# Last stage of two Fourier layers on one core: tile copies and plane loads issued by GpSimd's queue instead of the sync engine's

## The reference, cut to what matters

```python
# layer 0: 16 x 16 Fourier modes, plus a 1x1 skip
out_ft[..., :16, :16, :] = einsum('bxyi,xyio->bxyo', rfftn(x)[..., :16, :16, :], w)
x = x + irfftn(out_ft) + x_normed @ skip_kernel + skip_bias
# layer 1: 32 x 32 modes, two blocks of weights, then W, b and a relu
out = irfft2(blocks(rfft2(x_normed)[:, :, :32, :32], fw1, fw2))
x = x + relu(out @ W + b + out)
```

## Time and profile before

| | us |
|---|---|
| median of 3 runs | 2585.34 (2583.07 to 2605.12) |
| the profiled execution | 2589.53 |
| its span | 2587.7 |
| last stage, from the issue of its first planes to the span's end | 1413.07 to 2587.7 |
| PE busy, whole span | 1895.8 (73%) |
| DVE busy | 1411.1 (55%) |
| ACT busy | 1144.9 (44%) |
| POOL busy | 193.5 (7%) |
| share of the 16 DMA engines on SP's queue, whole span / last stage | 74.5% / 77.8% |

### The profile page before, as it was taken

One profiled execution on the slowest core, in us unless ns is written; L12 is line 12 of the kernel. 1 busy time (PEld: TensorE's weight loads), 2 busy tenths in 40 slices (PEclk: granted clock), 3 DMA queues, 4 the chain that ended last, 5 costly groups with the idle time before them and its releaser, 6 DMA issues. The chain is left out here.

```text
span 2587.7 us, 56902 instructions
## 1 busy us (share of the span) xinstructions
PE 1895.8 (73%) x22186; PEld 1516.2 (59%) x22186; DVE 1411.1 (55%) x2087; ACT 1144.9 (44%) x1884; POOL 193.5 (7%) x214
## 2 busy tenths in 40 slices
PE   4788887888389222122353699999988999988999
PEld 3566665667357122122352577777777777777877
DVE  5666665664144300000343577777776777767787
ACT  4555555553023100000231565656655655556665
POOL 0000000000100210011000120200102020200100
PEclk9999989999555566666676899999999999999999
DMA  7767766772765999999554487887878888887887
GB/s 268 241 218 225 228 222 213 231 239 75 160 80 69 194 220 226 228 227 214 164 195 150 144 297 269 284 288 238 264 263 286 275 284 269 291 279 246 268 294 291
DMA packets 318702, 589.74 MB, mean 228 GB/s; under 512 B 68806, under 2 KB 243362, under 8 KB 281634
## 3 DMA queue, kind: packets, MB, share of 16 engines
q1 hardware_dynamic: 264194, 562.51, 74.5%
q10 hardware_dynamic: 53504, 20.99, 3.6%
q0 software_dynamic: 736, 2.56, 0.3%
HBM read 380.99 MB, written 168.30 MB: 212 GB/s over the span
## 5 line engine op out<-in xcount | busy, mean ns | idle before, releaser
L1236 ACT ACTIVATE x_turned<-ps_xt 128x512 f16<-128x512 f32 x512 | 305.7, 597 | 418.9 <-PE ps_xt L1324 418.9
L1279 DVE TENSOR_TENSOR x_turned<-ps_xt,x_turned 128x512 f16<-128x512 f32 x512 | 350.7, 685 | 178.7 <-ACT x_turned L1236 178.7
L1368 PE MATMUL ps_y<-apply,x_turned 128*128 (+1 forms) x6144 | 434.7, 221 | 0.0
L1368 PEld LDWEIGHTS ps_y<-apply,x_turned 128*128 128x128 f16 x6144 | 384.1, 99 | 70.2 <-issue 7.8
L1324 PE MATMUL ps_xt<-c_eye,x_in 128*128 128x128 f32 x2048 | 321.4, 281 | 76.7 <-DMA x_in<-in_x 49.2
L220 DVE TENSOR_TENSOR parts<-stage,parts 128x1024 f16<-128x1024 f32 x256 | 304.3, 1220 | 126.9 <-ACT parts L144 126.4
L1300 DVE SCALAR_TENSOR_TENSOR y_out<-ps_y,relu 128x512 f32<-128x512 f32 x512 | 350.6, 685 | 30.2 <-PE ps_y L1368 12.6
L1246 ACT ACTIVATE relu<-ps_wave 128x512 f32<-128x512 f32 x512 | 303.1, 592 | 20.8 <-PE ps_wave L1354 20.7
L290 PE MATMUL row_ps<-parts,c_rows_dft 128*64 128x512 f16 x1536 | 216.4, 423 | 124.9 <-DVE parts L220 118.7
L144 ACT ACTIVATE parts<-stage 128x1024 f16<-128x1024 f32 x256 | 255.3, 1049 | 76.1 <-issue 37.6
L1324 PEld LDWEIGHTS ps_xt<-c_eye,x_in 128*128 128x128 f32 x2048 | 222.5, 144 | 80.3 <-DMA x_in<-in_x 41.8
(11 more groups left out here) (117 smaller groups left out, 2020.4 us busy)
## 6 DMA issues: line engine op xcount, KB each, us to landing
stage<-in_x SPq DMA_DIRECT2D x256, 512.0 KB, 4.5
x_in<-in_x SPq DMA_DIRECT2D x128, 1024.0 KB, 9.5
out_y<-y_out SPq DMA_DIRECT2D x128, 1024.0 KB, 5.0
fw_first<-in_fw SPq DMA_DIRECT2D x16, 2048.0 KB, 29.3
fw<-in_fw SPq DMA_DIRECT2D x16, 2048.0 KB, 29.3
mixed<-mix_out ACTq DMA_DIRECT2D x256, 64.0 KB, 6.7
raw<-mixed SPq DMA_DIRECT2D x16, 1024.0 KB, 6.6
planes_in<-planes SPq DMA_DIRECT2D x8, 1536.0 KB, 16.7
```

Source lines behind the costliest of these rows:

```text
L1236: nc.scalar.activation(turned[u % 2][:, 0, :, :], ps_turn[u % 2][:, :, :], ACT.Copy).then_inc(turn_high, 1)
L1279: nc.vector.tensor_tensor(v[:, 1, :, :], ps_turn[u % 2][:, :, :], v[:, 0, :, :], ALU.subtract).then_inc(turn_split, 1)
L1368: mm = nc.tensor.matmul(ps_y[u % 2][:, :, 2 * k:2 * k + 2], turned[u % 2][:, p, k, :], apply[:, bass.ds(b, 1), q, :, :].rearrange("p o c w ...
```

## The change

`load_planes` and `fill_tiles` move from SP's program to GpSimd's. SP keeps only the stores of y and the loads of x. GpSimd's program becomes, for each image b: wait for the last column group of the image before, fill the tiles of its block 1, turn the planes of b, load the planes of b + 1, fill the tiles of b's block 0. GpSimd's first load of planes has no wait; the starting value 1 that SP gave to `planes_turned` is gone, and PE's wait counts one less. The DMAs themselves (sources, targets, sizes, number) are the same.

```diff
-            def load_planes(b):
-                v = planes[bass.ds(b, 1)].rearrange("o q g y k c -> (o q g y) k c")
-                sp.wait_ge(planes_turned, PARTS_2 * b + 1)
-                sp.dma_start(D[:, :, :], v).then_inc(planes_landed, 16)
-
-            def fill_tiles(b, t):
-                sp.wait_ge(col_taken, group_number(b, t, GROUPS_2 - 1) + 3)
...
-                    sp.dma_start(dst, src).then_inc(tiles_filled, 16)
-
             def image(b, last):
                 for ch in range(CHUNKS):
...
-                    if (ch + 1) * UNITS == GROUPS_2:
-                        fill_tiles(b, 1)
-                        if not last:
-                            load_planes(b + 1)
-                    if (ch + 1) * UNITS == UB + GROUPS_2 and not last:
-                        fill_tiles(b + 1, 0)
             for i in range(Y_SLOTS):
                 sp.sem_inc(y_stored[i], 1)
-            sp.sem_inc(planes_turned, 1)
-            load_planes(0)
             for n in range(X_SLOTS):
                 load(0, n)
-            fill_tiles(0, 0)
...
         @block.gpsimd
         def _(pool):
-            pool.wait_ge(planes_turned, 1)
+            def load_planes(b):
+                if b > 0:
+                    pool.wait_ge(planes_turned, PARTS_2 * b)
+                pool.dma_start(D[:, :, :], planes[b].rearrange("q g y k c -> (q g y) k c")).then_inc(planes_landed, 16)
+
+            def fill_tiles(b, t):
+                pool.wait_ge(col_taken, group_number(b, t, GROUPS_2 - 1) + 3)
...
+                    pool.dma_start(dst, src).then_inc(tiles_filled, 16)
+
+            load_planes(0)
             for b in range(B):
-                pool.wait_ge(planes_landed, 16 * (b + 1))
                 if b > 0:
                     pool.wait_ge(col_ready, group_number(b - 1, BLOCKS - 1, GROUPS_2 - 1) + 1)
+                    fill_tiles(b - 1, 1)
+                pool.wait_ge(planes_landed, 16 * (b + 1))
                 for n in range(PARTS_2):
...
+                if b + 1 < B:
+                    load_planes(b + 1)
+                fill_tiles(b, 0)
+            fill_tiles(B - 1, 1)
...
-                    pe.wait_ge(planes_turned, PARTS_2 * b + g // TURN_GROUPS + 2)
+                    pe.wait_ge(planes_turned, PARTS_2 * b + g // TURN_GROUPS + 1)
```

More of the change, by code:

```diff
@@ L1213, in _ @@
         def _(pool):
-            pool.wait_ge(planes_turned, 1)
+            def load_planes(b):
[4 more added lines that the diff above has]
+                pool.wait_ge(col_taken, group_number(b, t, GROUPS_2 - 1) + 3)
+                high, low, zero = high_tile[t], low_tile[t], tile_0[t]
+                for dst, src in ((low[AGAIN:], high[SIN_1:ROWS_1]),
+                                 (zero[0:EVEN], high[COS_0:COS_0 + EVEN]),
+                                 (zero[EVEN:R0], high[COS_0 + EVEN:ROWS]),
+                                 (zero[R0:R0 + EVEN], low[COS_0:COS_0 + EVEN]),
+                                 (zero[R0 + EVEN:2 * R0], low[COS_0 + EVEN:ROWS]),
+                                 (zero[2 * R0:], high[COS_0 + 1:ROWS])):
+                    pool.dma_start(dst, src).then_inc(tiles_filled, 16)
+            load_planes(0)
             for b in range(B):
-                pool.wait_ge(planes_landed, 16 * (b + 1))
                 if b > 0:
                     pool.wait_ge(col_ready, group_number(b - 1, BLOCKS - 1, GROUPS_2 - 1) + 1)
+                    fill_tiles(b - 1, 1)
+                pool.wait_ge(planes_landed, 16 * (b + 1))
                 for n in range(PARTS_2):
```

## The result

The changed kernel is slower: 2625.8 us median (2619.61 to 2637.34, 4 runs) against 2587.09 us for the kernel before in the same comparison (2583.07 to 2605.12, 4 runs). The ratio is 1.0143, with a 95% interval of 1.0102 to 1.0184. Its profiled execution took 2630.59 us with a span of 2628.8. The prediction was 2539 us, in a range of 2508 to 2584.

The account below looks back on a forecast made before the run. The prediction took the order of DMA work within units 16 to 31 to stall PE. Its terms, -51 + 0 + 2 + 3 = -46 us, taken off the median of 2585.34, gave 2539 us, range 2508 to 2584.

Parts of the forecast that it names:

- What bounds the kernel: Last stage: DMA order within units 16 to 31 stalls PE, 68.2 us in seven stretches of images 0 to 6.
- The baseline of 28.23 us: Undisturbed length of 16 units without columns, read from units 32 to 47 of image 7 at full clock.
- SP without copies and planes: SP's store of chunk 4 and load behind it would issue seven us earlier, at 0.35 us an issue.
- Planes later: Units 16 to 31: planes issued at about 1513.5 instead of 1502.97, taking 3.7 us of work from ahead of chunk 8's load.
- The natural experiment: Units 16 to 31 of image 7, with copies, loads and stores but no planes to load, took 28.75 us against 37.97.
- Copies on another queue: Copies and x loads take turns by packet; residue 2.5 us a stretch, so units 16 to 31 change by -51 us.
- Units 48 to 63: Stretches with copies but no planes, in images 0 to 6: no change, with -17 and +18 us as ends.
- Image 7: Units 16 to 31 of the last image, where no planes are loaded: +2 us.
- Start: First planes share the engines with four x loads and GpSimd's queue starts late: +3 us, from nothing to +6.
- Rival C: 16 KB copy packets shut out chunk 7's load at unit 28's transpose; copies over 16 us erase the gain; chance 0.11.
- residue of 2.5 us: Wait assumed left in each of the seven stretches of units 16 to 31 after the change, between 0 and some 5.
- the forecast: Whole kernel: -46 us, to 2539 us off the median, own range 2510 to 2560; chance 0.60.

Follow-up runs that it names:

- e8: Kernel before the change, copies and planes still on SP, each load issued ahead of the store and earlier, SP's loop written out: 2515.2 us, ratio 0.968.
- e13: e8 with the image loops also written out on TensorE, ScalarE and VectorE, so no engine jumps back: 2462.8 us, ratio 0.955 to the kernel before.
- e4: Changed kernel with SP's load issued ahead of the store and before the chunk is done, SP's loop written out: 2514.2 us, ratio 0.974 to the kernel before.
- e1: Kernel before with only the planes loads moved to GpSimd's queue, copies left on SP: 2578.6 us, ratio 0.997.
- e6: Changed kernel with each copy split into two DMAs of every other 4 KB of the rows: 2542.7 us, ratio 0.978 to the kernel before.
- e5: Changed kernel with GpSimd's copies spaced one per unit after the first fill: 2537.5 us, ratio 0.975 to the kernel before.
- e12: Changed kernel with SP's load put ahead of the store, no earlier issue, SP's loop written out: 2516.8 us, ratio 0.976 to the kernel before.
- e11: Changed kernel with GpSimd's copies issued only once the load of chunk 7 or 15 has landed: 2536.4 us, ratio 0.981 to the kernel before.
- e10: Changed kernel with copies from image 1 on cut to one sixteenth of each row, not a usable kernel: 2502.3 us, ratio 0.969 to the kernel before.

## Why the prediction was wrong

*What bounds the kernel: right.* The waits of these stretches were worth about what I had read from the windows: 68 us in the earlier trace rows and at most 17 in the earlier trace rows; e8 took 61.6 and 10.2 out. The baseline of 28.23 us was 0.95 too low for images 0 to 6, since a stretch that ends in unit 32 with its first columns takes 29.18. The jump's price, 6.4 us a stretch, is shown by e13.

*SP without copies and planes: half right.* The store and the load of chunk 4 were issued on time, at 1507.16 and 1507.79 instead of 7 us late. But SP was held at that load for 4.56 us, not 0.35: of the three transfers that it had issued since the copies began (1500.72, 1501.35 and 1507.16) none had landed. And an early issue did not help a load that took 24.8 us to land where it had taken 15.8. The Trainium skill (DMA: Bandwidth & Descriptors, section Issuing engines are not separate DMA queues) says that issuing from several engines saves only the sequencer's time. The trace agrees as to the gain, and that saved time was worth nothing here (e4 against e8). By that rule the time would have stayed, and it rose by 1.4%.

*Planes later: right for the place, wrong as a cause.* Issued at 1520.21, behind turning, the planes cost nearly nothing: the six stretches of units 16 to 31 with them take 36.56 us, image 6's without them 36.39. But the gain that I booked against the planes was lost at another load. e1 shows that planes on a queue of their own, issued 4.7 us earlier in the stretch than that, still delay chunk 8. The natural experiment of the earlier trace rows was read rightly (no planes, no stall) and used wrongly: planes elsewhere are not planes absent.

*Copies on another queue: the step that failed.* The sum added the two works, 12.3 us of copies and 5 of the store and the load, and had the load of chunk 7 land at 1512.3, that is 17.5 us after its issue at 1494.77, against a need at 1511.95, with 2.5 us of wait a stretch taken on top. Measured, it landed 22.6 us after its issue, the wait was 5.34 us, and with the slower clock behind it a stretch lost 8 us (image 7: 36.24 against 28.23). Two terms were mis-sized. First, sharing cost more than the two works added: in 1508 to 1524 SP's queue had 0.493 x 16 x 16 = 126 us of engine time for 1.96 MB, that is 239 packets of 8 KB (the row also counts small ones), 0.53 us each, where alone they take 0.31 by the prediction's estimate. Nor was it turn about by packet: beside those 239 GpSimd's queue moved 1.25 MB, 76 packets of 16 KB. The earlier trace rows could not tell turns by packet from shares by bytes, since both queues' packets had nearly the same mean size there (0.57 MB in 120, 0.50 in 116). Second, I gave the copies nothing for starting first, ahead of a load that stood behind a store. In SP's order the load of chunk 7 had been issued *ahead* of the copies, and the old order protected it: 9.3 us to land. The diff does not touch that load, and it is the one that was hurt.

*Units 48 to 63: the same step, and the larger loss.* Here there was no gain from the planes to set against it. I took 0 and named +18 as the end; it was +36.8. Image 7 was +7.5 where I had +2.

*Start: right in sign, 4.3 us for 3.* The first turning began at 1427.47, 10.8 us after the planes' issue, instead of 7.0.

*Rival C, which I gave 0.11, is what happened*, in its place (the load of chunk 7, the transposes of units 28 and 60) and nearly at its price: 15 stretches, copies that take more than 16 us mixed (the last was issued at 1503.00 and landed 21.2 us later, at 1524.2). Its threshold stood in the text 0.4 us from my own sum (1512.3 against 1511.95). A margin that is gone in the sum itself is no ground for a residue of 2.5 us and a chance of 0.60; with both loads due within 2 us of their estimate, C and the forecast were about equally likely.

What stays open: why x packets beside copies take 1.7 times as long, and by what rule two queues share the engines. e6 (packets of 4 KB) and e5 (copies spaced and later) both remove the wait at unit 28, and each changed more than one thing. How much the queue that started first moves before the other begins was about 0.6 MB in e12, 1.6 to 1.8 in e11 and 1.8 in e5, and was not varied by itself.

## What to carry to other kernels

A queue's order is also a protection: before DMAs are moved to a queue of their own, list every transfer that stood ahead of them, and compute when it lands if it must now share. Where two transfers are issued together and only one has an engine waiting for it, that one goes first: swapping a load and a store on SP was worth 3 to 4% (e8 against the kernel before, e12 against the changed one), the change of queue beside it nothing. And where a sum comes out within a microsecond of its deadline, the case that misses it deserves as much chance as the case that meets it.

## What the runs showed of the hardware

- Small differences of issue decide which of two queues moves first. Copies issued on GpSimd's queue 0.2 us ahead of a store on SP's moved first (changed kernel, 0.51 MB against 0.14 in 1500 to 1504); issued 0.06 us ahead of a load they moved nothing for 3 us (e12, units 16 to 31); issued 0.7 us behind the second of two transfers of 1.05 MB they moved nothing for 5 us (e11).
- Beside the copies, the first of a store and a load on SP's queue landed after 11.3 or 11.5 us and the second after 22.6 or 20.0, whichever of the two it was (changed kernel, e12).
- A DMA issue took 0.34 us of SP's time with few transfers before it, and 4.56 us at 1507.79 in the changed kernel, where SP's last three transfers had not landed beside GpSimd's copies. GpSimd's six issues of that fill took 0.5 us each.
- SBUF to SBUF copies of 15 to 32 partition rows ran far under the rate of loads: 2.03 MB took 12.3 us of all 16 engines (share 0.77 over 16 us), where by the same rows' 424 GB/s 1.05 MB of x take an estimated 2.5.
- The jump back of the loop cost TensorE 4.6 us of waiting in the kernel before, 3.6 in the changed one and 3.1 in e10, and 1 to 2 us more where the granted clock of the stretch fell to 0.90 to 0.96 (e8, e10). Written out, the six stretches took 38.3 us less (e13).
